# ScalarE applies SiLU to the last even tile of the feed-forward part one step earlier

## What is computed

```python
q = jnp.einsum('btd,ed->bte', hidden_states, W_q)
sim = jnp.einsum('pbthn,hkpn->pbthk', q, keys)
scores_xy, idx_xy = jax.lax.top_k(sim, K)
...
scores, pk = jax.lax.top_k(all_scores, K)
indices = jnp.take_along_axis(all_idx, pk, axis=-1)
de = down_embed[indices]
ue = up_embed[indices]
w = jax.nn.silu(jnp.einsum('btd,bthkd->bthk', hidden_states, de) * jax.nn.softmax(scores, axis=-1))
experts_states = jnp.einsum('bthk,bthkd->btd', w, ue)
dense = jnp.einsum('bti,di->btd', jax.nn.silu(jnp.einsum('btd,id->bti', hidden_states, W_up)), W_down)
return dense + experts_states
```

## Time and profile before

| | us |
|---|---|
| median of 3 runs | 1224.01 (1223.81 to 1225.67) |
| the profiled execution | 1221.08 |
| its span | 1219.8 |
| feed-forward part, last two tiles, to the last layer norm's transposes | about 405 to 446 within the span |

### The profile page before, as it was taken

How to read it: one execution, slowest core, us unless ns; L and a number is a source line. 1 busy time by engine, 2 the same in 40 slices (tenths; PEclk the granted TensorE clock), 3 DMA queues, 4 the chain that set the end, 5 groups by cost and what they waited for, 6 DMA issues and landing times.

```text
span 1219.8 us, 23134 instructions
## 1 busy us (share of the span) xinstructions
PE 1101.7 (90%) x7614; PEld 797.0 (65%) x7614; DVE 956.9 (78%) x3336; ACT 671.3 (55%) x1732; POOL 444.0 (36%) x720
## 2 busy tenths in 40 slices
PE   0877778999998858999999999999999999999997
PEld 0775634666666645677776777777777776656666
DVE  1596968999998638978888878888888889755767
ACT  0220135555555516776777777677776688754441
POOL 0425332322221213544444444444444456423310
PEclk9997988999999979999999999999999999999999
DMA  9100030000000000000000000000000000000000
GB/s 274 44 1 1 1 104 1 1 1 1 1 1 1 1 0 1 2 2 1 1 2 1 1 1 1 2 1 2 2 1 2 1 2 2 1 1 5 7 10 16
DMA packets 19956, 15.32 MB, mean 13 GB/s; under 512 B 2432, under 2 KB 18816, under 8 KB 19712
## 3 DMA queue, kind: packets, MB, share of 16 engines
q1 hardware_dynamic: 19840, 13.86, 3.9%
HBM read 12.81 MB, written 1.05 MB: 11 GB/s over the span
## 4 chain that ended last, share of the span: by engine, by line
PE 70%; DVE 15%; issue 6%; ACT 5%; POOL 3%; DMA 1%; SPq 0%; DVEq 0%; POOLq 0%
PE bank L1468 11%; PE bank L1498 10%; PE bank L1462 10%; PE bank L1418 7%; PE bank L1776 5%; PE bank L972 4%; PE bank L1797 4%; PE bank L1438 3%; PE bank L1446 3%; PE bank L957 2%; ACT prb L1524 2%; DVE prob L1247 2%; DVE xm_e L722 1%; PE bank L932 1%; PE bank L950 1%
## 5 line engine op out<-in xcount | busy, mean ns | idle before, releaser
L1550 POOL TENSOR_SCALAR prb<-prb,rnorm 128x512 f32<-128x512 f32 (+3 forms) x512 | 273.1, 550 | 343.0 <-DVE rnorm L1628 342.9
L1524 ACT ACTIVATE prb<-prb,negmax 128x512 f32<-128x512 f32 (+3 forms) x512 | 281.0, 553 | 110.4 <-DVE negmax L1610 110.4
L1610 DVE CUSTOM_DVE_ANT_0 prb<-bank,mask 128x512 f32<-128x512 f32 (+3 forms) x512 | 218.7, 483 | 18.4 <-PE bank L1462 18.4
L1468 PE MATMUL bank<-ident,prb 128*128 128x128 f32 x1280 | 159.1, 276 | 6.0 <-POOL prb L1550 5.3
L1468 PEld LDWEIGHTS bank<-ident,prb 128*128 128x128 f32 x1280 | 139.5, 141 | 26.7 <-POOL prb L1550 14.8
L1498 PE MATMUL bank<-prbT,vv 128*64 128x512 f32 (+3 forms) x1024 | 151.9, 439 | 0.0
L1498 PEld LDWEIGHTS bank<-prbT,vv 128*64 128x64 f32 x1024 | 63.4, 136 | 82.3 <-issue 82.1
L1532 ACT ACTIVATE prbT<-bank 128x512 f32<-128x512 f32 x128 | 76.4, 597 | 62.1 <-PE bank L1468 61.6
L1619 DVE COPY prbT<-bank 128x512 f32<-128x512 f32 x128 | 87.7, 689 | 15.0 <-PE bank L1468 14.6
L1524 ACT ACTIVATION_READ_ACCUMULATOR prb<-prb,negmax 128x1 f32 x512 | 97.1, 190 | 0.0
L1834 ACT ACTIVATE h<-bank,eb1T 128x512 f32<-128x512 f32 x64 | 43.7, 686 | 53.9 <-PE bank L1776 53.7
(11 more groups left out here) (443 smaller groups left out, 2390.5 us busy)
## 6 DMA issues: line engine op xcount, KB each, us to landing
x<-in_x SPq DMA_DIRECT2D x2, 512.0 KB, 5.9
ew2T<-in_ew2T SPq DMA_DIRECT2D x1, 1024.0 KB, 8.3
ew<-in_ew SPq DMA_DIRECT2D x1, 1024.0 KB, 5.8
wq<-in_Wq SPq DMA_DIRECT2D x2, 512.0 KB, 5.2
wk<-in_Wk SPq DMA_DIRECT2D x2, 512.0 KB, 7.7
wv<-in_Wv SPq DMA_DIRECT2D x1, 1024.0 KB, 8.2
out<-res SPq DMA_DIRECT2D x16, 64.0 KB, 1.5
wmod<-in_wmod SPq DMA_DIRECT2D x2, 384.0 KB, 5.9
```

Source lines behind the costliest of these rows:

```text
L1468: last = T.transpose(into[:, at + (qc - kc) * P:at + (qc - kc + 1) * P], prb[j % 2][:, i, p_at[qc] + kc * P:p_at[qc] + (kc + 1) * P], iden ...
L1524: A.activation(v, v, ACT.Exp, scale=-1.0, bias=negmax[j % 2][:, place[qc], i:i + 1], accum_out=rowsum[j % 2][:, place[qc], i:i + 1]).then_ ...
L1550: last = G.tensor_scalar(v, v, rnorm[j % 2][:, place[qc], i:i + 1], 1.0, ALU.mult, ALU.mult)
L1610: V.tensor_tensor_reduce(prb[j % 2][:, i, p_at[qc]:p_at[qc] + (qc + 1) * P], s_of(j, s, i, qc), mask[:, (NT - 1 - qc) * P:S], 1.0, LARGEST ...
```

## The change

In an even step with no tile n+2, which is step 14 alone, ScalarE does the three SiLU instructions of tile 14 at the end of that step, behind `keep_sums(13)`. In step 15 they are left out where they stood. All other steps, engines, buffers and semaphore values stay as they are.

```diff
@@ -1094,10 +1094,15 @@
                         keep_sums(n - 1)
                     if n + 2 < TILES:
                         keep_sim(n + 2)
+                    else:
+                        silu_past(n)
+                        silu(n, 0)
+                        silu(n, 1)
                 else:
-                    silu_past(n - 1)
-                    silu(n - 1, 0)
-                    silu(n - 1, 1)
+                    if n + 1 < TILES:
+                        silu_past(n - 1)
+                        silu(n - 1, 0)
+                        silu(n - 1, 1)
                     for b, c in up_at(n):
                         silu_up(b, c)
                     if n + 2 < TILES:
```

## The result

| | before | changed |
|---|---|---|
| median of 18 runs each, us | 1224.33 | 1218.88 |
| lowest to highest | 1220.25 to 1227.47 | 1215.83 to 1221.24 |
| the profiled execution, us (span) | 1221.08 (1219.8) | 1219.23 (1217.9) |

The ratio is 0.9957, 95% interval 0.9946 to 0.9968, so the change takes 5.3 us off (3.9 to 6.6). The forecast was 5.8 us and 1218.2.

The account below looks back on a forecast made before the run. TensorE's sums(14) waits 4.25 us for ScalarE's SiLUs, then runs at a low clock. Earlier start 3.3 plus clock 2.5 gives 5.8 us off the median 1224.01, so 1218.2; range 1215.2 to 1221.6.

Parts of the forecast that it names:

- 6. `experts(14)`: TensorE: experts(14) follows dense(14) by 0.89 us as before, at 424.2 against 429.96, a shift of 5.8 us.
- Steps 1 and 2: ScalarE, step 14: tile 14's SiLUs end at 413.47; added table loads make tile 15's code, rank and gates 1.09 us later.
- Step 3: TensorE: sums(14) needs nothing more from ScalarE and starts at 419.4 in place of 422.67, 3.3 us gained.
- Step 4: TensorE's clock stays up behind a hole of about 1.1 us; sums(14)'s 32 matmuls take 3.84 against 6.34, gaining 2.5 us.
- Step 5: ScalarE: silu(15, 0) ends at 423.35, keep_sums(14) starts at 423.5; thin cover, each microsecond of later tile 15 gates costs one.
- Step 7's loose term: From the last layer norm into attention's first projections: when the low clock returns may differ, 1 us either way, zero in sum.
- the dear switch: Rival, ScalarE: each added table switch costs about another load, 2.6 us together; gain 3.2, time 1220.8; 5%.
- The clock that stays low: Rival, TensorE: the clock falls anyway and sums(14) still takes 6.34 us; gain 3.3, time 1220.7; 10%.
- the SiLUs did not matter: Rival: tile 14's SiLUs were hidden behind another late thing; gain under 2.4 us, time about 1223; 8%.
- The slower case: Rival, TensorE from rank(15, 0) on: the clock falls in the new hole and stays low; 9.4 us slower, 1233.4; 4%.

Follow-up runs that it names:

- e2: Changed kernel plus a one-column Exp and a one-column SiLU behind silu(14, 1), so two more table switches in step 14: 1223.84 us, ratio to before 1.0.
- e1: Kernel before, with 32 transposes into an unread bank on TensorE between rank(15, 3) and sums(14): 1220.63 us, ratio to before 0.9985.
- e3: Changed kernel with silu_past(14) and silu(14, 0) moved ahead of keep_sums(13), silu(14, 0) waiting for its own two heads alone: 1217.60 us, ratio to before 0.9952.
- e5: Changed kernel plus filler transposes on TensorE, 40 behind experts(15) and 30 behind the last transposes: 1218.65 us, ratio to before 0.9958.
- e7: Kernel doing the SiLUs of every even tile in that tile's own step, the change for all eight pairs: 1224.48 us, ratio to before 1.0003.
- e6: Changed kernel with silu_past(14) and silu(14, 0) ahead of keep_sums(13), sums(15) ahead of dense(15), and filler transposes in TensorE's two long holes: 1214.25 us, ratio to before 0.9923.
- e4: The e3 kernel, with sums(15) put ahead of dense(15) on TensorE after the loop: 1216.93 us, ratio to before 0.9945.

## Why the prediction was right, step by step

The numbers of the changed kernel below are less 4.04 us, the distance between the two starts of `sums(13)`.

| step | forecast | changed kernel |
|---|---|---|
| 1. SiLUs of tile 14 end | 413.47 | 413.48 |
| 2. copy of tile 15's code | 415.37 | 415.38 |
| 2. `rank(15, 0)` | 415.91 | 415.91 |
| 2. first gate of tile 15 | 416.66 | 416.66 |
| 3. `sums(14)` starts | 419.4 | 419.37 |
| 4. its 32 matmuls | 3.84 us | 3.73 us |
| 5. `keep_sums(14)` | 423.5 | 423.36 |
| 6. `experts(14)` | 424.2 | 424.05 |
| 7. transposes L908 | 439.3 | 439.20 |

Steps 1 and 2 held because every piece of them stood in the trace before, at the head of step 14; the price of a switch was its load alone, which e2 confirms with 3.00 us for two and the two small activations between them. Step 3 held as a wait of a known length. Step 4 was the risk: half of the gain hung on a clock that should not fall in a hole of about a microsecond. It did not, and e1 shows the term by itself, 2.53 against 2.5 forecast. I took the row with the hole (3.84), and the value without one (3.73) was nearer; this is the 0.1 us between 5.8 and 5.9. That the clock held was the likelier case of the forecast, not a certain one, and the last section shows holes only somewhat longer behind which it came out either way. Step 5 said that `silu(15, 0)` and `keep_sums(14)` meet within 0.2 us. In the trace the copy starts 0.02 us before the SiLU's modelled end, and 0.20 us after `dense(14)`, as before: it just fits. That each microsecond by which the gates come later would cost one is not shown: in e2 the gates came later, but so did `dense(14)`, and 0.68 us of slack opened there.

Step 7's loose term came out near zero for the changed kernel. From L908 to the first transposes of attention's probabilities it takes 24.71 us, 24.73 before. In e3 the same piece took 25.18 us (439.96 to 465.14), and its second group of projections ran at the low clock for longer (0.63 us each up to 451.2), so the term exists, with half a microsecond there. e5 shows that the low clock in this place is worth 1.7 us of this piece if it is avoided.

The measured gain, 5.3 us (3.9 to 6.6), holds the 5.9 of the trace. Of the rivals, the dear switch falls with e2. The clock that stays low falls with the trace. That the SiLUs did not matter falls with the start of `sums(14)`, 3.3 us earlier. The slower case would have needed a clock that falls in the new hole and does not return; e2 shows one that fell once the hole was about 3.9 us long, and there it was back at about 425.3, within the `rank` and `logit` matmuls, and cost 1.65.

What the prediction did not see is that its sum could be bettered by the same means: ScalarE stood idle 3.4 us ahead of `keep_sums(13)`, in the earlier trace rows, and the SiLUs fit there.

## What to carry to other kernels

Follow the last tile of a pipelined loop by itself: work that a steady step covers stands in the open there, and an order that is right for the loop can be wrong for its end: the same edit that gains at the end loses in every other pair (e7). When an engine's function tables must change, count both added loads and put them into time in which the engine waits; they are free there and cost their full length beside it. When a wait ahead of TensorE goes, look at the clock behind it: here 2.5 of 5.9 us came from matmuls that no longer ran at 1.2 GHz.

## What the runs showed of the hardware

Single executions of the same kernel scatter by 7 us (before: 1220.25 to 1227.47). The granted clock goes with it: of the 48 executions of the kernel before beside the experiments, the 18 with a mean clock of 0.976 or more took 1220.3 to 1222.3 us, the 27 with 0.974 or less 1222.9 to 1226.8. The traces say where part of it arises, in front of anything that was edited. The 32 matmuls L625 of the setup took 4.11 us in the profile of before and 6.51 in that of the changed kernel, behind the same wait for VectorE:

```profile
153.02 4.11 PE L625 MATMUL bank<-xm_b,ew2T 128*128 128x128 f32 x32 [2.55 <-DVE xm_b L731]
```

```profile
154.50 6.51 PE L625 MATMUL bank<-xm_b,ew2T 128*128 128x128 f32 x32 [2.55 <-DVE xm_b L731]
```

Over all traces these matmuls took 4.1 us three times, 5.5 four times and 6.5 twice, always behind a hole of 2.55 us. The same goes for `sums(12)`, 3.73 us in the profile of before (at 392.96) and 5.36 in that of the changed kernel (at 395.38), both behind a hole of 2.86 us ahead of L932; in the second the granted clock was 1.00 up to 395 and 0.61 behind it, so it fell when TensorE was at work again:

```profile
395.00:398.00 3.00, 3.00 (x16) 2.81 (x15) 3.00 (x14) 1.89 (x4) 0.68 (x2) 0.61 0.00 0
```

The code ahead of these places is the same in all these kernels, so I put the difference down to the execution; no kernel has two traces that would show it directly. Of the eight traces in which step 13 is the same, before, e5 and e6 have both groups short, the changed kernel and e1 to e4 both long. The first transposes also started 1.2 us later (35.76 against 34.55), since GpSimd's instructions ahead of them (L760) began as much later (32.56 against 31.35); what held those back the profile does not name.

So a forecast that rests on the clock behind a hole of 2.5 to 2.9 us has two right answers. The holes of 0.5 to 0.9 us at the place of the change left it at 1.00 in every trace here. The one of 4.25 us (before) and the one of about 3.9 us (e2) did not.
